# Attention projections cut into 64-row tiles and issued between the heads of a transformer layer on one core

## The reference

```
xn  = layernorm(x)
q,k = rms_norm(xn @ Wq.T), rms_norm(xn @ Wk.T)      # 16 heads of 16
v   = xn @ Wv.T
att = softmax(q k^T / 4) v                           # per batch and head
out = x + att @ Wo.T + ffn(xn)
```

## Time and profile before

| | |
|---|---|
| time, median of 3 runs | 1091.94 us (1089.85 to 1092.05) |
| span of the profiled execution | 1088.8 us |
| start up to the first heads | 0 to 35 us |
| attention, periods 0 to 117 | 35 to 642 us |
| last ten periods, change to the experts | 642 to 696 us |
| experts | 696 to 1088.8 us |
| busy share of the span | PE 96%, DVE 77%, ACT 68%, POOL 66% |
| granted clock of PE, mean | 0.994 |

### The profile page before, as it was taken

How to read it: one execution, slowest core, us unless ns; L and a number is a source line. 1 busy time by engine, 2 the same in 40 slices (tenths; PEclk the granted TensorE clock), 3 DMA queues, 4 the chain that set the end, 5 groups by cost and what they waited for, 6 DMA issues and landing times.

```text
span 1088.8 us, 20796 instructions
## 1 busy us (share of the span) xinstructions
PE 1040.4 (96%) x7222; PEld 673.1 (62%) x7222; DVE 838.4 (77%) x1893; ACT 745.1 (68%) x966; POOL 713.8 (66%) x753
## 2 busy tenths in 40 slices
PE   4899999999999999999999998999999999999997
PEld 3445555444454444445445443579988899998897
DVE  8999886787888878787888778677768777776861
ACT  3688888888787887888878886764546555455550
POOL 5677888577666766677676656546675576766434
PEclk9999999999999999999999999999999999999999
DMA  4544743443542543634533545234435243443313
GB/s 155 190 158 144 254 155 119 169 161 104 175 149 98 187 143 107 204 117 141 170 116 118 194 158 168 74 98 88 110 73 129 51 110 84 96 123 57 64 20 39
DMA packets 83530, 138.15 MB, mean 127 GB/s; under 512 B 9936, under 2 KB 35792, under 8 KB 83408
## 3 DMA queue, kind: packets, MB, share of 16 engines
q1 hardware_dynamic: 54560, 103.05, 28.0%
q0 software_dynamic: 12288, 16.79, 9.2%
q10 hardware_dynamic: 16560, 16.78, 4.7%
HBM read 86.25 MB, written 50.33 MB: 125 GB/s over the span
## 4 chain that ended last, share of the span: by engine, by line
PE 75%; DVE 12%; issue 5%; ACT 4%; POOL 2%; ACTq 1%; another core or an unknown queue 0%; POOLq 0%; DVEq 0%
PE W L1480 16%; PE S L1466 15%; PE pv L509 14%; PE S L494 11%; PE W L453 9%; PE W L464 3%; ACT prob L710 3%; PE W L478 3%; DVE xb L787 1%; PE R L423 1%; DVE ge L937 1%; DVE raw L842 1%; PE R L1452 1%; PE pv L1452 1%; ACT lg L690 1%
## 5 line engine op out<-in xcount | busy, mean ns | idle before, releaser
L710 ACT ACTIVATE prob<-S 128x1024 f32<-128x1024 f32 x512 | 498.2, 1022 | 111.6 <-PE S L494 110.8
L509 PE MATMUL pv<-prob,v 128*17 128x512 f32 x2048 | 247.2, 596 | 1.9 <-DVE oT L875 1.7
L494 PE MATMUL S<-stq,stk 64*128 64x512 f32 x1024 | 200.9, 456 | 10.5 <-ACT prob L710 7.3
L494 PEld LDWEIGHTS S<-stq,stk 64*128 64x128 f32 x1024 | 84.2, 184 | 140.5 <-ACT prob L710 108.5
L1742 POOL DMA_INDIRECT out<-prob,order_rows x64 | 105.7, 1652 | 48.1 <-DVE prob L1682 37.1
L509 PEld LDWEIGHTS pv<-prob,v 128*17 128x17 f32 x2048 | 46.3, 96 | 117.7 <-issue 116.3
L1205 POOL TENSOR_TENSOR sq<-raw 128x512 f32<-128x512 f32 x62 | 64.5, 1042 | 81.9 <-DVE raw L842 56.6
L1542 ACT ACTIVATE wq_act<-S,b 128x512 f32<-128x512 f32 x64 | 43.8, 687 | 94.6 <-PE S L1466 88.9
L1466 PE MATMUL S<-raw_nT,xT_w 128*128 128x512 f32 x384 | 91.1, 395 | 0.0
L1235 POOL TENSOR_TENSOR lo<-full,hi 128x512 fp32r<-128x512 f32 x62 | 80.1, 1292 | 5.0
L1466 PEld LDWEIGHTS S<-raw_nT,xT_w 128*128 128x128 f32 x384 | 71.6, 188 | 17.7 <-issue 1.7
(11 more groups left out here) (257 smaller groups left out, 2592.1 us busy)
## 6 DMA issues: line engine op xcount, KB each, us to landing
stk<-parts SPq DMA_DIRECT2D x93, 256.0 KB, 3.5
stq<-parts SPq DMA_DIRECT2D x93, 256.0 KB, 4.4
xT<-in_w SPq DMA_DIRECT2D x32, 512.0 KB
parts<-hi SPq DMA_DIRECT2D x63, 256.0 KB, 2.1
parts<-lo SPq DMA_DIRECT2D x63, 256.0 KB, 2.1
out<-ao ACTq DMA_DIRECT2D x32, 256.0 KB, 3.5
xb<-in_x ACTq DMA_DIRECT2D x13, 512.0 KB, 4.0
xb<-in_x SPq DMA_DIRECT2D x2, 512.0 KB, 5.4
```

What stands on the lines that cost most here:

```text
L494: ins = e.matmul(S[n % 2][:, h, :], stack["k"][u][64 * h:64 * h + 64, p, c * P:(c + 1) * P], stack["q"][u][64 * h:64 * h + 64, p, :], star ...
L509: ins = e.matmul(pv[32 * j:32 * j + VW, :], v[b % 2][:, c, 8 * u + 4 * g + j, :], prob[(2 * t + j // 2) % RING][:, j % 2, :], start=(c == ...
L710: e.activation(prob[n % RING][:, :, :], S[n % 2][:, :, :], ACT.Exp).then_inc(s_exp, 1)
```

## The change

- In periods before the last ten each matmul of a projection is cut in two halves of 64 rows, which use the two row halves of the array side by side as the heads do, with 256 moving columns each. One turn of six such pairs sums the upper rows for one bank of W and the lower rows for the other, and a second turn the other way round. A projection fills the first 256 columns of both banks. The second turn waits on a new semaphore `s_half` until the first is done.
- The order on PE becomes: head 0, first turn, head 1, second turn, heads 2 and 3, scoring of x, both weighings, counting matmuls, turning of x.
- The matmuls of the choice of experts are cut into four column tiles of 32 (`over`).
- W now holds one projection, so it is drained in its own period: `turn_raw` and `copy_v` move one period earlier and, on DVE, behind `moments` and `norm_x` and ahead of `keep_score`; `evict_o` moves from periods 5 and 6 to 4 and 5, between third and fourth exponential. The first turn waits for the drain of the projection before.
- `denominators` and `divide` move from even periods to the odd ones behind them, and to the front of DVE's list; `turn_o` follows a period after.
- `prob` has seven buffers instead of six. Many small tiles share memory with others to make room, and the constant `iota` is loaded later.
- In the last ten periods heads and weighings keep their order but for small moves, and projections stand between heads 1, 2 and the second weighing.
- `POOL`'s places for `split_x` and `split_qk`, and the places of the projections over a batch, are as before.

```diff
-RING = 6
+RING = 7
+LEAN = PERIODS * (B - 1) - 2
+HALF = N // 2
...
+def fills(at):
+    return sum(1 for t in range(at) if not (t in (4, 5) or t >= PERIODS * (B - 1) - 2 and t % PERIODS not in (4, 5)))
+
+def divided_at(n):
+    at = 2 * n + 2
+    return at if at >= LEAN else at + 1
+
+def turned_at(n):
+    return divided_at(2 * n + 1) + 1
...
-    W = [ps(f"W{i}", [P, N]) for i in range(2)]
+    W = ps("W", [P, 2, N])
+    filled = W[:, :, 0:HALF]
...
+    def in_rows(e, at, turn, kept, moved):
+        if turn:
+            e.wait_ge(s_half, fills(at) + 1)
+        for j in range(6):
+            for h in range(2):
+                c, rows = h ^ turn, slice(64 * h, 64 * h + 64)
+                ins = e.matmul(W[:, c, 0:HALF], kept(j, c)[rows], moved(j, c)[rows],
+                               start=(j == 0 and not turn), stop=(j == 5 and turn == 1))
+        if not turn:
+            ins.then_inc(s_half, 1)
+        return ins
...
+    def project_qk(e, nb, i, at, turn):
+        u, n = i // 2, "qk"[i % 2]
+        if turn == 0:
+            e.wait_ge(s_xl, 2 * nb + 2)
+            if i:
+                e.wait_ge(s_raw, 4 * nb + i)
+            elif nb >= 3:
+                e.wait_ge(s_ao, 2 * (nb - 3) + 2)
+            else:
+                e.wait_ge(s_v, 2 * (nb - 1) + 2)
+        ins = in_rows(e, at, turn, lambda j, c: w[n][PRODUCTS[j % 3][0]][:, j // 3, u * P:(u + 1) * P],
+                      lambda j, c: (xh, xl)[PRODUCTS[j % 3][1]][nb % 2][:, j // 3, HALF * c:HALF * (c + 1)])
+        if turn:
+            ins.then_inc(s_proj, 1)
...
+    def project_o(e, b, i, at, turn):
+        if turn == 0:
+            e.wait_ge(s_onl, 2 * b + 2)
+            if i == 0 and b + 2 < B:
+                e.wait_ge(s_v, 2 * (b + 2) + 2)
+            else:
+                e.wait_ge(s_ao, 2 * b + i)
...
                 heads(e, b, 4 * kk)
+                if at >= LEAN:
...
+                else:
+                    fill(e, at, 0)
                     heads(e, b, 4 * kk + 1)
+                    fill(e, at, 1)
                     heads(e, b, 4 * kk + 2)
+                    heads(e, b, 4 * kk + 3)
+                    if scored(at - 3) is not None:
+                        score_x(e, scored(at - 3))
+                    if at:
+                        weigh(e, 2 * at - 2)
+                        weigh(e, 2 * at - 1)
+                    if ex is not None and (ex < E - 1 or i == 0):
+                        route_tensor(e, ex, i)
+                    if scored(at - 1) is not None:
+                        turn_x(e, scored(at - 1), 0)
+                    if scored(at - 2) is not None:
+                        turn_x(e, scored(at - 2), 1)
...
+    def over(e, to, n, kept, moved):
+        for j in range(4):
+            ins = e.matmul(R[32 * j:32 * j + 32, to:to + n], kept[:, 32 * j:32 * j + 32], moved, start=True, stop=True)
+        return ins
```

More of the change, by code:

```diff
@@ L1100, in vector_program @@
                 ex, i = routed(at)
+                for n in range(4 * B):
+                    if divided_at(n) == at and at < LEAN:
+                        denominators(e, n // 4, n % 4)
                 if at == ROUTE:
@@ L1117, in vector_program @@
                     place_rest(e)
-                for m in (nb, nb + 1):
-                    for i in range(4):
-                        if m < B and qk_at(m, i) + 1 == at:
-                            turn_raw(e, m, i)
                 if scored(at) is not None and at:
@@ L1126, in vector_program @@
                     second_variance(e, scored(at - 1))
+                for m in (nb, nb + 1):
+                    for i in range(4):
+                        if m < B and qk_at(m, i) == at:
+                            turn_raw(e, m, i)
+                for i in range(2):
+                    if nb < B and v_at(nb, i) == at:
+                        copy_v(e, nb, i)
                 if scored(at - 3) is not None:
@@ L1289, in gpsimd_program @@
                             square(e, m, i)
+                for n in range(4 * B):
+                    if divided_at(n) == at and kk < 2:
+                        divide(e, n // 4, n % 4)
                 if b and kk == 0:
-                    divide(e, b - 1, 3)
                     split_o(e, b - 1, 0)
@@ L1300, in gpsimd_program @@
                         x["gather"](e, 0, c)
-                if kk in (2, 4, 6):
-                    divide(e, b, kk // 2 - 1)
+                for n in range(4 * B):
+                    if divided_at(n) == at and kk >= 2:
+                        divide(e, n // 4, n % 4)
                 if b and kk == 3:
@@ L1375, in experts @@
     xscale = [sb(f"e_xc{u}", [P, CH]) for u in range(G)]
-    xshift = [sb(f"e_xs{u}", [P, CH]) for u in range(G)]
-    one = sb("e_one", [P, CH])
-    minus = sb("e_minus", [P, CH])
+    xshift = t["veps"] + t["var2"]
+    one, minus = (spare[:, 16 * G + CH * i:16 * G + CH * (i + 1)] for i in range(2))
     up = [t["S"][i // 2][:, i % 2, :] for i in range(UP)]
```

207 lines of the change are left out of this document (120 added, 87 removed).

## The result

| | before | after |
|---|---|---|
| time, median (4 runs each, taken together) | 1090.89 us (1086.44 to 1092.05) | 1108.05 us (1106.77 to 1108.08) |
| span of the profiled execution | 1088.8 us | 1106.3 us |
| start up to the first heads | 35.3 | 35.3 |
| periods 0 to 31 | 175.9 | 193.0 |
| periods 32 to 117 | 431.2 | 437.7 |

The ratio is 1.0168, with a 95% interval of 1.0143 to 1.0193: slower by some 17 us, where 30.5 were forecast. The stages are counted from first head to first head, so 32 to 117 ends 2.6 us later here than in the earlier trace rows. Up to period 117 the trace after is 23.6 us longer (17.1 + 6.5); the last stage gives 6.1 back, and that is not the change's doing (see 8).

A forecast was written before the change was run, and what follows sets the result against it. PE, 96% busy, bounds the kernel; the new order makes a ring with ACT. Ring 2, inverse norms 5.5, early turning periods 8, late operands 9 + 3 + 3: 30.5 on the 1088.8 span, 1119.3, plus 3.1: 1122.5 us; range 1102 to 1147.

The forecast's parts named there:

- the ring: Plain period: head, two exponentials on ACT, fourth head, both weighings on PE wait in turn; 4.84 us against 4.79 before.
- rival (a): Only the ring and the switches count, the three late operands mostly absorbed: +8 to +17, 1100 to 1109 us; chance 0.17.
- late operands: First 32 periods: projections moved to the front wait for xl, onl and DVE's work in period 3; +15 us.
- inverse norms, 21 periods: Every fourth period: ACT's inverse norms between first and second exponential lengthen the period to 5.34 us; +5.5 in all.
- xl, periods 6, 14, 22: Next q and k projection waits for POOL's split of x, 3.7 us into the period: +3.1 x 3 = +9.
- onl, periods 12 and 20: Output projection, period 4 of batches 1 and 2, waits for onl, ready 2 us into the period: +1.6 x 2 = +3.
- normalisation 4.62: DVE's normalisation of x in period 3 of a batch, taken as 4.62 us, part of it overlap with POOL.
- Covered, at nothing: Plain period: DVE drains W by 3.7 to 4.2 us, before 4.95, so the next projection's wait costs nothing.
- (b): PE alone sets the time, a plain period takes 4.42 us: about -27, 1065 us; chance 0.10.
- (c): No difference: a plain period of about 4.6 us pays for the early stalls; chance 0.04.
- milder form with 0.14 a pair: Each pair of 64-row matmuls takes 0.14 us instead of 0.12: +0.12 x 118 = +14; chance 0.03.
- (d): Weight loads of 64-row pairs not hidden: 0.23 us a pair, period 5.7, about +110, 1205 us; chance 0.04.

The follow-up runs named there:

- 8: The kernel before, run again unchanged: one run of 1088.3 us, its neighbour 1092.31; period 118 to the end took 445.2 us.
- the late pad: Changed kernel plus a small unused ACT operation between third and fourth exponential in 59 plain periods: 1113.06 us, against 1112.43 without it on the same chip.

## Why the prediction was right, and where its sizes were off

**The direction and the ring held.** Forecast slower by 30.5; measured 17.2 between medians, 17.5 between spans. 1108.05 lies inside 1102 to 1147, but 14 below the likeliest value and at the upper end of rival (a), "ring only, late operands mostly absorbed". Some 6 of the 14 are luck: the last stage, where the change does little, came out short in the trace after and long in the trace before. Up to period 117 the change cost 23.6, between rival (a) and the forecast. The spans split like this:

| term | forecast | measured |
|---|---|---|
| plain period | 4.79 to 4.84; +2 over 65 | 4.84; +2.0 over 50 |
| inverse norms, 21 periods | 5.34; +5.5 | 5.34; +4.3 (they took 5.13 before, on the mean) |
| the other early periods | +0.3 each, 28: +8 | +0.26 each on the mean, 24: +6.2 |
| xl, periods 6, 14, 22 | +3.1 each: +9 | +0.1, +2.7, +1.6: +4.4 |
| onl, periods 12 and 20 | +1.6 each: +3 | +0.65 each: +1.3 (the turning's +0.26 included) |
| DVE in period 3 | +0.9 each: +3 | nothing beyond the +0.26 |
| periods 0, 4 and 5 | as the others | +2.1, +1.3, +1.8: +5.2 |
| periods 32 and 33 | as the others | +2.3 |
| 13 periods of the choice of experts | nothing | -2.1 |
| from period 118 | nothing | -6.1 |

The measured terms add to 17.5. For the early periods the prediction's own lines give 5.54 - 5.19 = 0.35, so +10 for 28 and not +8. Of the -2.1, 1.9 is period 99 alone, which took 6.70 in the trace before and 5.39 in that of the kernel before again. No run took out the shared tiles, the seventh buffer or the late constant, which the prediction put at nothing.

**Which step was mis-sized.** The late operands, by the term "normalisation 4.62". The prediction copied it from one period where POOL worked beside all four operations. It noted that part of it was overlap, and took off nothing like enough. The change moves POOL's scaling of q and k earlier, so in period 11 only the first of the four overlaps, and they take 1.97. The transpose of the scores is then not late at all (+0.9 forecast, 0 measured). The variance and POOL's second power come earlier, onl is ready 0.6 us into its period instead of 2.0 (109.56 in a period begun at 108.94), and xl 2.4 instead of 3.7 (123.14 in one begun at 120.72). The Trainium skill (SBUF — State Buffer, "SBUF: two separate sides") says that a GpSimd operation and a VectorE operation in a two-port mode, or with two inputs in SBUF, share one pair of ports as an exclusive lock: whoever starts second stands still for the whole instruction. The trace agrees: an operation takes 0.40 with POOL idle (the median after) and up to 1.46 where it starts behind one of POOL's, and all 64 of them took 54.2 us before and 32.7 after. How much of the rest of the gap is each operand's new place in POOL's queue was not tried apart.

**What was missed.** "Covered, at nothing" for the drain of W failed in period 0 (+2.1). There DVE has the moments of x ahead of the drain, and the new order wants W at once (chain of waits):

```profile
36.00 1.42 DVE st L860 x4
...
37.94 0.73 DVE raw L930
...
38.80 1.65 PE W L469 x12
```

That is the wait of 3.0 for `raw`. Period 4 was counted as one of the 28, but batch 0 has no output projection. The old order took only 4.13 without one; the new order is held by the ring and takes the 5.45 of its neighbours (+1.3).

An idle stretch on PE also had a second price, which no step of the forecast had: the half clock behind it. Period 5 with it took 7.51 instead of 5.93 (period 13), so 1.6 more; period 14 8.70 instead of 7.67 (period 22), 1.0 more; period 33 6.28 instead of 5.13 (period 81), 1.1 more. But the 1.6 is not a price on top. The trace with the late pad is the changed kernel's order up to period 40 and had no half clock in period 5. There period 5 took 5.89 and period 6 took 7.37, with a wait of 1.7 for xl (PE's waits from 66 to 85 us):

```profile
PE W L469 <- POOL xl L1299: 1.7, 1, 1.7
```

The two together took 13.26, against 7.51 + 5.96 = 13.47. So the half clock in period 5 hid the lateness of xl behind it: the +0.1 in the table does not show that xl was in time in period 6, and the three half clocks cost some 2.3 net (0.2 + 1.0 + 1.1). In the same trace the clock fell in period 22 (8.72) and not in 14 (7.66), and not in 33 (5.19). Which of these stretches of idle time is followed by it changes from one execution to the next; why stays open.

**The last stretch.** Its -6.1 is not the change's: 396.6 - 391.8 = 4.8 of it is the late signal of the last output projection, which both programs have in some executions. The other 1.3 lie in periods 118 to 126, which took 49.9 in the kernel before, 48.6 in it again, and 48.6 in the changed kernel.

**The rivals.** (b), PE alone at 4.42, is out: a plain period takes 4.84, PE idles 0.25 of it for the exponential, and a pad on ACT lengthens it. Its 4.42 for PE's own work was too small as well: 4.84 - 0.25 = 4.59, of which 0.09 is the second turn's wait. (c), no difference, is out by the ratio. The milder form with 0.14 a pair is out, for a pair takes 0.12. (d), loads not hidden, is out too: a pair comes every 0.12 us, and the period is 4.84, not 5.7. The Trainium skill (TensorE: Matmul & The Clock Gate, Part 3, mechanism) ties the overlap of a weight load to a different row group; here pairs on the same two row groups follow at 0.12 us with their loads, so this case's trace disagrees.

**The signs named ahead.** PE idles some 0.3 us ahead of the fourth head in a plain period: 0.25. ACT idle about 1 us: 0.89. Pairs 0.12 apart: yes. PE waiting 3 us for xl in periods 6, 14 and 22: 2.0, in two of them.

## What to carry to other kernels

A period in which two engines hand work back and forth can be set by the ring, not by the busier engine: draw the ring of the new order before counting what a cheaper instruction mix saves, and find out with a small pad on the other engine which part of a period has no slack (here 0.12 us of period for 0.14 us of pad on one side, none on the other). Work moved to the front of an in-order queue shows every operand that was late before, and the idle time it makes can be paid a second time in clock, or hide the next wait. Compare stage by stage before crediting a difference to the change: a stage that the change leaves alone may differ by 5 us from one execution to the next. A duration read where two engines share something holds only beside the same neighbour: take its shortest and longest value from the trace as the two bounds.

## What the runs showed that was not expected

- Gains for PE were lent, not kept. Taking 7.3 us out of the periods 2 and 6 of the kernel before (32 to 117) changed nothing (1.0002).
- A DVE operation on 128x1 values (`best`) takes 0.16 us alone; the longest in the changed kernel took 1.19. One like it, at 299.25, took 1.18 and ended at 300.43, as POOL's operation of 299.13 to 300.41 did.
- A switch into a whole-array tile behind the weighings costs 0.10 us on this path, not 0.2.
- PE's second turn loses 0.09 us at its start, read as its wait on PE's own semaphore, although the work waited for stands in the same queue with one head between.
- The first output of PE's last attention projection is signalled 2.6 to 4.2 us after its recorded end in nine of fourteen traces, and on time in five; that alone moves the whole time by 2 to 5 us.
